# A decoder block on one core: weights of the prologue in halves, and matmuls with unread results beside the first steps

## The reference

```
x = x + attention(layernorm(x), w_qkv, w_proj)     # part 1
x = x + long_convolution_mix(layernorm(x), k, bias, ctx, ctx)
x = x + gated_ffn(layernorm(x), gate_w, up_w, down_w, scales)

bitlinear(x, w): sx = 127 / max|x| of the row;  xq = round(x * sx) / sx
                 sw = 1 / mean|w|;              wq = clip(round(w * sw), -1, 1) / sw
                 xq @ wq.T
attention:       q, k, v = bitlinear(x, w_qkv), 16 heads of 32 channels
                 softmax(causal(q @ k.T / sqrt(32))) @ v, then bitlinear(out, w_proj)
```

## Time and profile before

| | before |
|---|---|
| profiled execution, its own time | 1488.82 us |
| its span, first to last instruction | 1487.0 us |
| mean granted TensorE clock | 0.982 |
| PE matmul busy | 1390.5 us (94%) |
| DVE busy | 1234.5 us (83%) |
| POOL busy | 1177.6 us (79%) |
| ACT busy | 871.8 us (59%) |
| DMA, share of 16 engines (largest queue) | 35.4% |

### The profile page before, as it was taken

The page is one execution under the profiler, slowest core; times in us unless marked ns, Lnnn a source line. Parts: engine busy times, 40 slices in busy tenths (PEclk is TensorE's granted clock), DMA queues, the critical chain, the costliest instruction groups (busy, mean ns, idle before and its releaser), DMA issues.

```text
span 1487.0 us, 23871 instructions
## 1 busy us (share of the span) xinstructions
PE 1390.5 (94%) x8327; PEld 775.5 (52%) x8405; DVE 1234.5 (83%) x1964; ACT 871.8 (59%) x1437; POOL 1177.6 (79%) x902
## 2 busy tenths in 40 slices
PE   3698999999986898899999999999999999999998
PEld 2577787878764443334444444444444444444443
DVE  6789999999984799789898899899889888888611
ACT  5589999999886223444545455455456446544341
POOL 3279999999985687888888878878887888788532
PEclk9799999999998899999999999999999999999999
DMA  5545565655431533222422331332323232240001
GB/s 191 132 111 152 139 167 139 167 139 152 127 83 58 175 100 81 68 50 71 100 50 52 91 78 43 79 78 64 78 64 71 62 81 50 68 102 15 18 19 29
DMA packets 171587, 133.57 MB, mean 90 GB/s; under 512 B 120500, under 2 KB 124748, under 8 KB 171468
## 3 DMA queue, kind: packets, MB, share of 16 engines
q1 hardware_dynamic: 171276, 131.91, 35.4%
q10 hardware_dynamic: 192, 0.14, 0.0%
HBM read 50.67 MB, written 19.92 MB: 47 GB/s over the span
## 4 chain that ended last, share of the span: by engine, by line
PE 64%; DVE 12%; POOL 8%; issue 7%; ACT 7%; DMA 1%; SPq 0%; POOLq 0%; DVEq 0%; ACTq 0%
PE gu L839 20%; PE gu L853 10%; PE shared_bank L784 9%; POOL pL L1782 3%; PE y L806 3%; PE y L800 3%; PE y L803 3%; PE y L808 3%; PE y L809 3%; DVE blockmax L980 2%; DVE o_sb L1020 2%; DVE z L1210 1%; DVE qkt L960 1%; PE s_kq L632 1%; ACT pH L1427 1%
## 5 line engine op out<-in xcount | busy, mean ns | idle before, releaser
L1654 ACT ACTIVATE shared<-shared_bank 128x512 f32<-128x512 f32 x162 | 96.1, 593 | 320.5 <-PE shared_bank L784 320.5
L1207 DVE TENSOR_TENSOR y<-shared,y 128x512 f32<-128x512 f32 x324 | 223.9, 691 | 41.2 <-ACT shared L1654 22.1
L1782 POOL TENSOR_TENSOR pL<-pT,pH 128x768 f16<-128x768 f32 x128 | 217.0, 1698 | 12.9 <-ACT pH L1427 7.4
L839 PE MATMUL gu<-fT,wg 128*128 128x512 f16 x768 | 181.4, 379 | 1.5 <-DMA fT<-fnl 1.5
L1214 DVE TENSOR_REDUCE oT<-z 128x64 f32<-128x512 f32 x256 | 175.6, 686 | 8.7
L839 PE MATMUL gu<-fT,wu 128*128 128x512 f16 x768 | 182.2, 380 | 0.0
L1210 DVE TENSOR_TENSOR z<-y,cT 128x512 f32<-128x512 f32 x236 | 162.3, 688 | 10.7 <-PE y L798 4.4
L1916 POOL TENSOR_TENSOR fuL<-fu,fuH 128x512 f16<-128x512 f32 x96 | 112.0, 1167 | 71.8 <-ACT fuH L1669 71.6
L853 PE MATMUL gu<-wd,fuL 128*128 128x512 f16 x384 | 145.6, 379 | 0.0
L853 PE MATMUL gu<-wd,fuH 128*128 128x512 f16 x384 | 145.6, 379 | 0.0
L1852 POOL TENSOR_TENSOR kv<-vT,cT 128x1024 f32<-128x1024 f32 x70 | 137.8, 1970 | 5.9 <-ACT vT L1609 5.9
(11 more groups left out here) (222 smaller groups left out, 3540.2 us busy)
## 6 DMA issues: line engine op xcount, KB each, us to landing
pack<-qkhl SPq DMA_DIRECT2D x256, 128.0 KB, 2.6
x_sb<-in_x SPq DMA_DIRECT2D x16, 512.0 KB, 4.0
c_sb<-in_ctx SPq DMA_DIRECT2D x32, 256.0 KB, 4.0
hankel<-in_L_xattn_k SPq DMA_DIRECT2D x32, 256.0 KB, 4.1
out_y<-yo SPq DMA_DIRECT2D x32, 256.0 KB, 2.9
x_grp<-x_scratch SPq DMA_DIRECT2D x30, 256.0 KB, 3.5
x_scratch<-x_sb SPq DMA_DIRECT2D x14, 512.0 KB, 3.0
wraw<-in_L_attn_w_qkv SPq DMA_DIRECT2D x3, 1024.0 KB, 9.6
```

The costliest lines, as they stand in the source:

```text
L839: made = T.matmul(bank[:], (wg, wu)[which][:, cb, ib * P:(ib + 1) * P], fT[:, cb, part, :], start=cb == 0 and part == 0, stop=cb == CB - 1 ...
L1207: chain.step(V.tensor_tensor(bank[:], shared[2 * part + half][:], bank[:], op))
L1782: G.tensor_tensor(pL[n % 2][:], pT[n % NP][:], pH[n % NP][:], ALU.subtract).then_inc(low_done, 1)
```

## The change

It has seven parts.

1. **Halves.** K becomes ternary on DVE in two halves of two blocks (ternary_k), Q on ACT in two halves (sign_weights with parts). PE turns K 0, 1, then Q 0, 1, does the first Q and the first K product, turns K 2, 3, does the second K product, turns Q 2, 3, does the second Q product. A product waits only for its own two blocks. ACT copies the first two Q blocks, DVE the last two.
2. **V on POOL.** ternary_v has the three passes, behind power_in(1); DVE's ternary(2) is gone.
3. **Projection magnitude** on ACT (magnitude(3, 0, 4)) instead of DVE; its total and scale are made in the prologue.
4. **Statistics.** stats_in(1) stands behind the first low parts, stats_in(2) and stats_in(3) in the prologue.
5. **Two steps later:** the turning of the projection weights (steps 2 and 4 instead of 1 and 2), and the first piece of the FFN weights (loads at step 5 instead of 3).
6. **Row maxima of batch 0** alternate between s_qk and s_kq, and wait for the pair before the last alone.
7. **Unread matmuls.** keep_warm(n) issues n matmuls of 512 columns into pv, which nothing has used yet: 24 behind the last product of batch 0, and 4 in each step from -1 to 7.

```diff
+        tern_pool = signal("tern_pool")
...
-        V_WEIGHTS_AT, PROJ_WEIGHTS_AT, LOAD_PIECES_AT = (-1, 0), (1, 2), 3
-        OUT_SCALE_AT, OUT_SIGN_AT = -1, 0
+        V_WEIGHTS_AT, PROJ_WEIGHTS_AT, LOAD_PIECES_AT = (-1, 0), (2, 4), 5
+        OUT_SIGN_AT = 0
+        WARM_FIRST, WARM_STEP = 24, 4
...
-            return n if k == (0 if n else 4) and 0 <= n < PIECES else None
+            return n if k == (0 if n else 6) and 0 <= n < PIECES else None
...
+        W_TURNS = [(1, 0), (1, 1), (0, 0), (0, 1), (1, 2), (1, 3), (0, 2), (0, 3)] + [(i, ob) for i in (2, 3) for ob in range(WB)]
...
-            return i == 0 or (i >= 2 and ob % 2 == 0)
+            return (i == 0 and ob < 2) or (i >= 2 and ob % 2 == 0)
...
-            return s % 2, 2 * (s // 2)
+            return ((0, 0), (1, 0), (1, 2), (0, 2))[s]
+
+        def score_tile(n):
+
+            return s_kq if n < PAIRS and n % 2 == 1 else s_qk
...
-                wT_ready(w, qk)
+                wT_ready(w, qk, (g0, g0 + 1))
...
-                w.wait_ge(max_done, n)
+                w.wait_ge(max_done, max(n - 1, 0) if n < PAIRS else n)
                 wait_packed(w, b)
+                to = score_tile(n)
...
+            def keep_warm(n):
+                for i in range(n):
+                    T.matmul(pv[:], ident_b[:], pick[:, 0:4, :], start=True, stop=True)
...
-            turn_weights(1)
-            turn_weights(0)
+            turn_weights(1, (0, 1))
             spread_c(0)
-            for g2 in range(4):
-                multiply_qk(0, g2)
+            turn_weights(0, (0, 1))
+            multiply_qk(0, 0)
+            multiply_qk(0, 1)
+            turn_weights(1, (2, 3))
+            multiply_qk(0, 2)
+            turn_weights(0, (2, 3))
+            multiply_qk(0, 3)
+            w.wait_ge(const_done, C_PART1)
+            keep_warm(WARM_FIRST)
+            weight_total(4, 1, 1)
...
+                if -1 <= t < PROB:
+                    keep_warm(WARM_STEP)
...
-                if t == OUT_SCALE_AT:
-                    weight_total(4, 1, 1)
...
-            ternary(1)
+            ternary_k(0)
+            ternary_k(1)
+            copy_weights(1, (0, 1))
...
-            copy_weights(1)
-            stats_in(1)
...
-            for g2 in range(4):
-                scale_qk(0, g2)
+            scale_qk(0, 0)
+            copy_weights(1, (2, 3))
+            scale_qk(0, 1)
+            copy_weights(0, (2, 3))
+            scale_qk(0, 2)
+            scale_qk(0, 3)
             for g2 in FIRST_LOW_ON_DVE:
                 low_first(g2)
+            stats_in(1)
+            stats_in(2)
             max_in(1)
             scale_in(1)
-            magnitude(3, WB, 4)
-            ternary(2)
+            weight_scale(1, 1, 2, 1)
+            w.wait_ge(wscale_done, 3)
+            chain.step(V.tensor_tensor(ws[:, 5:6], ws[:, 0:1], ws[:, 2:3], ALU.mult))
+            stats_in(3)
...
-            round_weights(0)
+            sign_weights(0, 0, slice(0, 2))
             diagonal(0)
-            sign_weights(0)
             for j in range(2):
                 copy_xqT(0, j)
-            copy_weights(0)
+            copy_weights(0, (0, 1))
             copy_c(0)
+            sign_weights(0, 1, slice(2, 4))
+            for g2 in range(4):
+                high_qk(0, g2)
+            magnitude(3, 0, 4)
             moments(1)
-            high_qk(0, 0)
...
+            def ternary_v():
+                w.wait_ge(wscale_done, 1)
+                chain.step(G.tensor_scalar(wraw[2][:], wraw[2][:], ws[:, 1:2], ROUND, ALU.mult, ALU.add))
+                chain.wait()
+                chain.step(G.tensor_scalar(wraw[2][:], wraw[2][:], ROUND - 1.0, ROUND + 1.0, ALU.max, ALU.min))
+                chain.wait()
+                w.wait_ge(wtr_pe, w_turned(0, WB - 1))
+                G.tensor_scalar(tern[0][:], wraw[2][:], ROUND, None, ALU.subtract).then_inc(tern_pool, 1)
...
             for g2 in range(4):
                 if g2 not in FIRST_LOW_ON_DVE:
                     low_qk(0, g2)
+            power_in(1)
+            ternary_v()
```

More of the change, by code:

```diff
@@ L364, in decoder_kernel, with wT_copied @@
         W_ORDER = (1, 0, 2, 3)
+        W_TURNS = [(1, 0), (1, 1), (0, 0), (0, 1), (1, 2), (1, 3), (0, 2), (0, 3)] + [(i, ob) for i in (2, 3) for ob in range(WB)]
         def wT_by_act(i, ob):
-            return i == 0 or (i >= 2 and ob % 2 == 0)
-        def wT_copies(i, ob, by_act):
-            done = W_ORDER[:W_ORDER.index(i)]
-            return (sum(wT_by_act(j, o) == by_act for j in done for o in range(WB))
-                    + sum(wT_by_act(i, o) == by_act for o in range(ob + 1)))
+            return (i == 0 and ob < 2) or (i >= 2 and ob % 2 == 0)
+        def wT_copied(i, ob):
+            by_act = wT_by_act(i, ob)
+            return sum(wT_by_act(*at) == by_act for at in W_TURNS[:W_TURNS.index((i, ob)) + 1])
         def w_turned(i, ob):
-            return WB * W_ORDER.index(i) + ob + 1
+            return W_TURNS.index((i, ob)) + 1
         def low_made(n):
@@ L391, in turning, with wT_ready @@
                     yield i, range(2 * at.index(t), 2 * at.index(t) + 2)
-        def wT_ready(w, i):
-            w.wait_ge(wT_act, wT_copies(i, WB - 1, True))
-            w.wait_ge(wT_dve, wT_copies(i, WB - 1, False))
+        def wT_ready(w, i, blocks=range(WB)):
+            for ob in blocks:
+                w.wait_ge(wT_act if wT_by_act(i, ob) else wT_dve, wT_copied(i, ob))
         def qk_groups(s):
-            return s % 2, 2 * (s // 2)
+            return ((0, 0), (1, 0), (1, 2), (0, 2))[s]
+        def score_tile(n):
+            return s_kq if n < PAIRS and n % 2 == 1 else s_qk
         def wait_packed(w, b):
@@ L546, in turn_weights @@
                 for ob in blocks:
-                    by_act = wT_by_act(i, ob)
                     w.wait_ge(const_done, C_BASE)
-                    bank = misc1.take(("wT", i, ob), w, (wT_act if by_act else wT_dve, wT_copies(i, ob, by_act)))[:].bitcast(BF16)
-                    if i in (1, 2):
-                        w.wait_ge(tern_dve, i)
+                    bank = misc1.take(("wT", i, ob), w, (wT_act if wT_by_act(i, ob) else wT_dve, wT_copied(i, ob)))[:].bitcast(BF16)
+                    if i == 1:
+                        w.wait_ge(tern_dve, ob // 2 + 1)
+                    elif i == 2:
+                        w.wait_ge(tern_pool, 1)
                     else:
-                        w.wait_ge(tern_act, 1 if i == 0 else 2)
+                        w.wait_ge(tern_act, ob // 2 + 1 if i == 0 else 3)
                     for cb in range(CB):
@@ L560, in weight_total @@
                 w.wait_ge(const_done, C_BASE)
-                w.wait_ge(wsum_dve, 2 + use)
-                w.wait_ge(wsum_act, 2)
+                w.wait_ge(wsum_dve, 2)
+                w.wait_ge(wsum_act, 2 + use)
                 T.matmul(bank[:, 0:n], ones[:], wsums[:, first:first + n], start=True, stop=True).then_inc(wtot_pe, 1)
@@ L926, in weight_scale, with ternary_k @@
                 V.reciprocal(ws[:, at + 1:at + 2], ws[:, at:at + 1]).then_inc(wscale_done, 1)
-            def ternary(i):
+            def ternary_k(half):
+                part = slice(2 * half, 2 * half + 2)
                 w.wait_ge(wscale_done, 1)
                 w.wait_ge(wsum_act, 2)
-                chain.step(V.tensor_scalar(wraw[i][:], wraw[i][:], ws[:, 1:2], ROUND, ALU.mult, ALU.add))
+                chain.step(V.tensor_scalar(wraw[1][:, part, :], wraw[1][:, part, :], ws[:, 1:2], ROUND, ALU.mult, ALU.add))
                 chain.wait()
-                chain.step(V.tensor_scalar(wraw[i][:], wraw[i][:], ROUND - 1.0, ROUND + 1.0, ALU.max, ALU.min))
+                chain.step(V.tensor_scalar(wraw[1][:, part, :], wraw[1][:, part, :], ROUND - 1.0, ROUND + 1.0, ALU.max, ALU.min))
                 chain.wait()
-                if i == 2:
-                    w.wait_ge(wtr_pe, w_turned(0, WB - 1))
-                V.tensor_scalar(tern[i % 2][:], wraw[i][:], ROUND, None, ALU.subtract).then_inc(tern_dve, 1)
+                V.tensor_scalar(tern[1][:, part, :], wraw[1][:, part, :], ROUND, None, ALU.subtract).then_inc(tern_dve, 1)
             def copy_weights(i, blocks=range(WB)):
@@ L1122, in vector_program @@
                     copy_weights(i, blocks)
-                if t == OUT_SCALE_AT + 1:
-                    weight_scale(1, 1, 2, 1)
-                    w.wait_ge(wscale_done, 3)
-                    chain.step(V.tensor_tensor(ws[:, 5:6], ws[:, 0:1], ws[:, 2:3], ALU.mult))
                 for use, k in halves(t):
@@ L1142, in vector_program @@
                 for b, k in batches(t, NORM_AT, LOAD_AHEAD + 11, 2):
-                    if k == LOAD_AHEAD:
+                    if k == LOAD_AHEAD and b > 3:
                         stats_in(b)
@@ L1801, in gpsimd_program @@
             set_once()
-            power_in(1)
             for g2 in range(4):
```

36 lines of the change are left out of this document (16 added, 20 removed).

## The result

The changed kernel took 1508.92 us, median of four runs (1508.05 to 1510.43), against 1488.96 (1487.70 to 1491.14) for the kernel before on the same chip: 1.0134 times, 95% interval 1.0116 to 1.0151. It is slower by 20 us. I had forecast 1490.7 and a range of 1485.5 to 1495.6.

What follows compares the result with a forecast made beforehand. It took mid part 1 as a full pipeline, so only its start, set in the first 90 us, counts: +4.3 - 1.6 - 1.3 - 0.1 = +1.3 us, giving 1490.7 on the median; range 1485.5 to 1495.6.

Steps and rivals of the forecast that it cites:

- Halves: Prologue: first products start 2 us earlier and end about 3.2 us later; low parts done at 35.5.
- the rival of a better overlap: Prologue: copies and scalings fall beside PE's pieces, low parts end at about 31.5, total 1485.7 us; chance 0.2.
- Batch 1: Prologue: its maximum at 41.4, PE's turn at 43.4, ACT's copy of c ended at 46.6, 7.3 us late.
- POOL's three passes: V weights, ahead of batch 2's power: 6.2 us taken, at no cost; upper end 14.2 us, costing 5.8.
- R0: PE's first row maxima (step 0): at 48.83 us in the kernel before, forecast at 52.4.
- The rival on POOL: POOL's V passes set batch 2's power: at 4.3 us a pass they cost 4.5, total 1495.2 us; chance 0.2.
- R0 to R2: PE from its first row maxima to step 2: forecast from 52.4 to 60.8, predicted 8.4 us.
- R2 to R8: PE from step 2 to step 8: forecast 15.45 us, 1.3 less than before.
- my third rival: Added matmuls don't keep the clock: R2 to R8 up to 3 us more, step 2 0.9; about 1493.5; chance 0.15.
- Unread matmuls: The 24 behind the first products cost nothing; the 4 in each step add 0.87 us of PE work.
- R8: PE's step 8, the first with probabilities: at 74.80 us in the kernel before, forecast near 76.
- The moved FFN piece: DVE's two passes (0.8 us each) move into steps 8 and 9: 9.05 us from R8 to step 11 against 9.19.

Runs made afterwards that it cites:

- e3: Changed kernel with the three passes over the V weights on DVE instead of POOL: 1503.3 us, 1.0092 of the kernel before.
- e4: Changed kernel with the first FFN piece back at its old steps and the V passes on DVE: 1493.1 us, 1.0028 of the kernel before.
- e5: e4 without the unread matmuls: 1495.0 us, 1.0035 of the kernel before.
- e9: Changed kernel with only the first FFN piece's sum, take and store back at their old steps: 1498.5 us, 1.0068 of the kernel before.
- e10: e9 and e3 together on the changed kernel: 1494.5 us, 1.0044 of the kernel before.
- e8: e4 with batch 1's statistics, moments and power earlier, projection turned and FFN pieces loaded at old steps: 1489.9 us, 1.0009 of the kernel before.
- e7: Kernel before with the unread matmuls alone added: 1488.9 us, 0.9996 of the kernel before.

## Why the prediction was wrong

- **Halves: right.** Low parts done at 35.09 (predicted 35.5), pack 0 issued 35.18 (35 to 36). The three banks serialise as worked out, and the rival of a better overlap is refuted.
- **Batch 1: right.** Its turn 43.00 (43.4), at the lower clock in spite of the 24 matmuls, ACT's copy of c 45.86, end 46.24 (46.6), its variance of batch 2 by 46.4.
- **POOL's three passes: mis-sized.** I took 6.2 and measured 14.6 (38.23 to 52.87). The power of batch 2 was then 5.9 late, and R0 58.38 for 52.4, ACT's projection pass 61.16 for 55.3. My upper bound of 14.2 came within 0.4 of it, by luck, as it was the price of another operation; what failed is the choice of the low end "as it too reads one input". The number of inputs was the wrong likeness: an affine select says nothing of maximum and minimum. The rival on POOL named the mechanism and priced it at 4.5.
- **R0 to R2 and R2 to R8: right as numbers, the first by help of the late POOL.** 8.28 (predicted 8.4) and 15.78 (15.45), granted clock 1.00 from 75 to 78 us. In e3 POOL is out of the way and ACT's projection pass stands at 54.99 (predicted 55.3), as in my sum. There PE waits 3.26 before batch 2's turn and comes out at the lower clock:

```profile
59.55 1.12 PE L586 MATMUL misc<-ident,xn 128*128 128x128 f32 x4 [3.26 <-ACT wqkvT L1431]
...
61.32 0.63 PE L619 MATMUL s_qk<-pack 128*128 128x256 f16 x2
```
```profile
60.00:62.00 2.00, 2.00 (x12) 1.75 (x11) 0.00 (x0) 1.15 (x4) 0.89 (x2) 0.50 0.88 204
```

  R0 to R2 then takes 9.24 and R2 to R8 16.27, 0.8 over my terms each. The first is my third rival (the added matmuls don't keep the clock over that gap) at about the 0.9 that I gave for R2; how much of the second is the clock was not separated.
- **Unread matmuls: no net cost, but not free.** Their 1.9 us before R8 and 1.6 us back behind it (e4 and e5) are two terms that I had as one of PE's pace; the medians show neither.
- **The moved FFN piece: the failed step.** "Its two passes over the first weight piece ... move two steps back, behind R8", and then "Both give the same to 0.1", counted DVE's two passes alone. A moved step takes along what it triggers: POOL's take went from step 16 to 18 and SP's store from 17 to 19, past the 16 transfers of step 18, while the mask of piece 2 stayed in step 18. The wait of 13.57 replaced one of about 1.8, and e9 puts it at 10.4 us. I put the effect behind step 11 at nothing and looked no further, though the piece's tasks reach to step 19 and the trace of the kernel before shows only 3.1 us between the store and that pack (102.67 and 105.76).

Sum: +1.3 forecast, +5.9 for POOL, +0.3 up to R8, +11.8 for the wait (13.57 less 1.8) give 19.3; measured 20.0. That they agree so well is in part luck: in the profiles the mask of piece 2 is 18.9 late, of which 1.8 is gained back by the third store, and 2.7 are lost behind part 1. With what the experiments gave back in place of the two large terms (5.6 and 10.4) the sum is 17.6, so 2.4 of the 20.0 stay unexplained. e3 and e9 together (e10) give back 14.4, not 16.0. What remains, 4 us in e4 and 6 in e10, is more than the 1.3 of my sum. In e3 R8 is 2.8 late against the kernel before, where I had 1.4; the difference is the two times 0.8 above, less 0.3 that R0 came early (52.08 for 52.4). In e8 R8 is 0.4 ahead of the kernel before; against e4 the new order in the prologue gives 3.5 us at R0 and the bundle of its edits 2.2 more up to R8.

## What to carry to other kernels

When a task that runs as a chain over several engines is moved by n steps, list every link at its new step and every queue that each link now stands behind, up to the last consumer, and compare with the next instance of the task that was not moved. Before work goes to another engine, take its price from a row with the same operation; where there is none, carry both bounds into the sum, since here the upper one came true. A term that keeps or raises the clock of one engine has to be priced by the steps in which another waits for that engine: the unread matmuls did keep the clock (e7), cost 1.9 us in some steps and gave 1.6 in others (e4 and e5), and the medians did not move.
